# Moving the weight loads of an attention and mixture-of-experts kernel from SyncE's queue to ACT's

## What is computed

```
x = x + attention(layernorm(x), ctx)        # q = ln(x) Wq + bq; k, v from ctx; ALiBi bias; softmax; Wo
g = softmax(layernorm(x) Wg + bg); top 2, renormalised
for e in range(8):
    h = gelu(ln(x) @ W1[e] + b1[e]);  out += (h @ W2[e] + b2[e]) * combine_w[:, e]
x = x + out
```

## Time and profile before

| | us |
|---|---|
| median of 3 runs (512.02 to 512.95) | 512.09 |
| the profiled execution | 508.91 |
| its span | 507.1 |
| PE busy in the span | 419.6 |
| DVE busy | 312.6 |
| ACT busy | 232.4 |
| POOL busy | 223.7 |

### The profile page before, as it was taken

The page is one execution under the profiler, slowest core; times in us unless marked ns, Lnnn a source line. Parts: engine busy times, 40 slices in busy tenths (PEclk is TensorE's granted clock), DMA queues, the critical chain, the costliest instruction groups (busy, mean ns, idle before and its releaser), DMA issues. The chain is left out here.

```text
span 507.1 us, 16158 instructions
## 1 busy us (share of the span) xinstructions
PE 419.6 (83%) x5137; PEld 330.3 (65%) x5138; DVE 312.6 (62%) x875; ACT 232.4 (46%) x607; POOL 223.7 (44%) x305
## 2 busy tenths in 40 slices
PE   5565768897888999995179899989989998999981
PEld 2554556676666778873168677668867876777760
DVE  5357848796778777554526466636664765566560
ACT  1333636564555564563234444534543553445430
POOL 3123528887888886677602222222222232122232
PEclk9865979898989999998579999989998999999997
DMA  6574455555646535333322223113222322122110
GB/s 225 134 229 150 139 152 189 175 175 192 215 136 185 165 123 163 122 123 127 127 64 37 39 41 53 35 29 45 46 44 31 53 38 43 34 43 47 22 12 0
DMA packets 52967, 50.70 MB, mean 100 GB/s; under 512 B 22672, under 2 KB 47024, under 8 KB 52784
## 3 DMA queue, kind: packets, MB, share of 16 engines
q1 hardware_dynamic: 45192, 41.07, 27.0%
q0 software_dynamic: 7152, 8.47, 9.9%
q10 hardware_dynamic: 576, 0.53, 0.3%
HBM read 33.73 MB, written 17.50 MB: 101 GB/s over the span
## 5 line engine op out<-in xcount | busy, mean ns | idle before, releaser
L976 PE MATMUL ps<-area,wts 128*128 128x128 f16 (+1 forms) x2896 | 197.0, 243 | 0.1
L976 PEld LDWEIGHTS ps<-area,wts 128*128 (+1 forms) x2896 | 157.5, 103 | 41.0 <-issue 2.1
L976 PE MATMUL ps<-wts,area 128*128 x624 | 153.4, 330 | 2.2 <-DVE area L934 1.8
L718 ACT ACTIVATE area<-ps,late 128x128 f32<-128x128 f32 x312 | 89.2, 368 | 115.0 <-PE ps L976 115.0
L932 DVE TENSOR_SCALAR area<-area 128x512 f16<-128x512 f32 x78 | 33.0, 424 | 77.8 <-ACT area L718 77.7
L976 PE MATMUL ps<-area 128*128 128x154 f16 (+2 forms) x928 | 71.0, 236 | 12.0 <-DMA area<-qd 11.1
L976 PEld LDWEIGHTS ps<-area 128*128 128x128 f16 (+1 forms) x928 | 59.8, 107 | 21.2 <-issue 8.1
L595 POOL DMA_INDIRECT out<-o,row_id x20 | 31.6, 1579 | 95.1 <-issue 65.0
L595 POOL DMA_INDIRECT out<-xn,row_id x19 | 30.0, 1579 | 92.4 <-issue 79.8
L804 DVE TENSOR_REDUCE mx<-ps 128x3 f32<-128x462 f32 (+1 forms) x96 | 53.1, 579 | 24.3 <-PE ps L976 23.9
L621 ACT ACTIVATE area<-ps 128x512 f32<-128x512 f32 x80 | 47.3, 595 | 27.7 <-PE ps L976 25.5
(11 more groups left out here) (121 smaller groups left out, 419.1 us busy)
## 6 DMA issues: line engine op xcount, KB each, us to landing
stage<-in_w SPq DMA_DIRECT2D x32, 512.0 KB, 5.0
area<-xlist SPq DMA_DIRECT2D x39, 130.0 KB, 2.0
area<-qd SPq DMA_DIRECT2D x16, 256.0 KB, 2.7
qd<-wts SPq DMA_DIRECT2D x48, 64.0 KB, 1.9
area<-in_x SPq DMA_DIRECT2D x16, 128.0 KB, 2.3
out<-area SPq DMA_DIRECT2D x16, 128.0 KB, 1.8
xlist<-pad_rows SPq DMA_DIRECT2D x11, 130.0 KB, 2.5
area<-in_b SPq DMA_DIRECT2D x1, 1024.0 KB, 5.0
```

The costliest lines, as they stand in the source:

```text
L718: last = nc.scalar.activation(h32[par][:, c * P:(c + 1) * P], h_ps[par][m][:, f * P:(f + 1) * P], ACT.Gelu_apprx_tanh, bias=b1T[:, ds(e * ...
L976: return nc.tensor.matmul(out_, lhsT, rhs, start=start, stop=stop, skip_group_check=skip)
```

## The change

All loads of weights, the output pack and the kink tables are issued by ACT instead of SP. `load_w` is the same function with `act` in place of `sp`. In the turns it stands at the end of ACT's turn, after the second weight split; before the first turn it stands after ACT's `query(0)`. SP keeps the x loads and stores, the hops and the spare rows.

```
 SP, before the first turn, and in turn(i):
-            for u in range(2):
-                load_w(u)
             load_x(3)
-            sp.dma_start(late[:], pack_o).then_inc(s.o_in, 16)
...
                     write_q(f2)
                     read_q(f2)
-                for u in weight_units(i + 1) if i > -3 else []:
-                    load_w(u)
                 if sc is not None:
                     write_m(sc)
-                if i == 2:
-                    sp.dma_start(kinks[:], kink_in).then_inc(s.kink_in, 16)
 ACT, in turn(i), and before the first turn:
+            def load_w(u):
+                e, second, n, place = u // 4, u % 4 // 2, u % 2, u % NSTAGE
+                wait(act, S[f"w_lo{place}"], u // NSTAGE)
+                if second:
+                    act.dma_start(staged(u), w2[e, n * 512:(n + 1) * 512, :].rearrange("(c p) d -> p c d", p=P)).then_inc(S[f"w_stage{place}"], 16)
+                else:
+                    act.dma_start(stage[:, place, :], w1[e, n * P:(n + 1) * P, :]).then_inc(S[f"w_stage{place}"], 16)
...
                 for u in units[1:2]:
                     split_w_hi(u)
+                for u in weight_units(i + 1) if i > -3 else []:
+                    load_w(u)
+                if i == 2:
+                    act.dma_start(kinks[:], kink_in).then_inc(s.kink_in, 16)
...
             query(0)
+            for u in range(2):
+                load_w(u)
+            act.dma_start(late[:], pack_o).then_inc(s.o_in, 16)
             for i in range(FIRST, LAST):
                 turn(i)
```

More of the change, by code:

```diff
@@ L374, in store @@
                 sp.dma_start(out_rows[ds(first_row(t), P), :], xr[:, t % 8, :]).then_inc(s.x2_out, 16)
[L376 to L382, removed]
             def write_q(t):
```

## The result

The changed kernel is slower. Its median is 526.37 us (4 runs, 520.29 to 526.68) beside 512.06 us for the kernel before (511.12 to 512.95): a ratio of 1.027 [1.021, 1.032]. The prediction was 507.2 us, in a range of 502.0 to 514.5. Run again later beside other kernels it came to 522.17 us (6 runs, 518.22 to 525.09), 1.018 [1.013, 1.023]. The profiled execution took 526.68 us, its span is 524.8 us.

What follows compares the result with a forecast made beforehand. Before the expert loop, TensorE waits for the queries' read-back, held up by slow `md` writes behind weight loads in SyncE's queue. Stall gains less added costs summed to -4.9 us: 512.09 becomes 507.2, range 502.0 to 514.5.

Steps and rivals of the forecast that it cites:

- Turn 2: Turn 2's scores: `md` lands in 3 us, the stall shrinks by 3.0 us and the low clock behind it by 2.0.
- ACT's issue time: Turns: two issues, about 0.9 us a turn, mostly covered by ACT's idle time, except at turn 14's start: +0.5.
- About 1 us does not [fit in]: +1.0: Start-up: most data of loads ACT issues earlier fits into free engine time before first scores; +1.0, bounds 0 and +4.
- rival 3: Start-up costs the full 4 us, time 510.2; chance 0.07.
- Early turns: 0: End of turn -2: units 2 and 3 issued beside the query read, offset by freer `qd` write; 0, bounds -1 and +1.5.
- Turn 6's stall: the same mechanism: -2.2: Turn 6's scores: a quicker `md` hop removes TensorE's wait as in turn 2; -2.2 us, bounds 0 and -3.
- The kink tables, "+0.3 at most": End of turn 2: one issue more on ACT, before a turn in which TensorE waits for POOL; +0.3 taken.
- Turn 16, "+0.8 (bounds 0 and +2.5)": Turn 16: units 30 and 31, issued late beside `b2`, delay ACT's split and the tail; +0.8.
- Rival 2: Every turn: loads collide with the `md` write, using up 2.7 us to spare; 523.9, or 519.4 at half the turns; chance 0.12.
- three signs of being wrong: Steady-turn `md` at 4 us or more, new `area<-qd` waits in turns 3 to 12, first scores after 26.5 us.
- rival 1: Hops keep their length because engines are full; 514.9, or 511.0 with half the stalls' time gone; chance 0.16.

Runs made afterwards that it cites:

- experiment 4: Kernel before with SyncE's weight loads issued behind the `md` write instead of ahead of it, nothing on ACT; 507.68 us, 0.994.
- experiment 10: Kernel before with only the two first weight loads and the output pack issued by ACT, after its first query copy; 515.46 us, 1.005.
- 5: Changed kernel with start-up loads, output pack and kink tables back on SyncE, units 30 and 31 issued by ACT a turn earlier; 516.92 us, 1.012.
- 9: Kernel 5 with the units of turns -1 and 0 issued by ACT at the start of their own turn; 513.46 us, 1.001.
- experiment 2: Changed kernel with only the kink tables issued by SyncE again, behind the maxima write of turn 2; 521.44 us, 1.019.
- experiment 7: Changed kernel with only units 30 and 31 issued by ACT at the end of turn 14 instead of 15; 519.91 us, 1.012.
- 6: Kernel 5 with units of turns -1 to 12 issued by ACT behind its xnT copy, later ones by SyncE behind the `md` write; 509.73 us, 0.994.
- 12: Kernel before, SyncE's loads both behind the `md` write in early turns; from turn 3 one ahead, one behind; 509.31 us, 0.995.

## Why the prediction was wrong

**What held.** *Turn 2.* The working gave `md` 3 us to land and took 5.0 us from turn 2 (3.0 for the stall, 2.0 for the clock). The hop took 3.03 us, the turn became 5.7 us shorter, and the granted clock of 66 to 73 us went to 1.00. The mechanism was right, and experiment 4 shows that it was had without a second queue. *ACT's issue time* was taken at +0.5 in turn 14 and cost nothing: ACT idles the same 0.32 us before it copies `o_sb` at 227.49 as it did before. The issues aren't in the engine's way, since they go out while earlier activations still run.

**What failed.** Under most of the steps lies one: that `md` and the other hops get through quickly once the loads are in another queue, whenever the loads leave. By the steps of the prediction:

- *"About 1 us does not [fit in]: +1.0"* for the start-up. It was 2.9 us in the trace and 2.4 us alone (experiment 10), rival 3's case more nearly. The step summed the free time of 14.6 to 24 us and let the loads fill it. But loads issued first aren't filler. They took the engines to 0.99 in 18 to 22 us, when the hops were out, and left 0.35 free in 22 to 27, when there was nothing left to hide.
- *"Early turns: 0"*. They cost 3.3 us in turns -1 and 0, about 1.0% by experiments 5 and 9. The step looked at the queue (query read beside loads, not behind them) and assumed that ACT issues at the end of its turn. It issues before its splits begin, in turn -2 beside the queries' writes, the first load 0.4 us ahead of them:

```profile
30.42 0.39 ACTq L606 DMA_DIRECT2D stage<-in_w  x1
30.69 1.05 ACT L600 ACTIVATE wts<-stage 128x1024 f16<-128x1024 f32 x1
30.82 0.89 SPq L382 DMA_DIRECT2D qd<-wts  x2
...
36.12 0.33 SPq L396 DMA_DIRECT2D area<-qd  x1
```

  From the last write's issue (31.76) to the read-back it takes 4.36 us; before, from 28.83 to 31.15, 2.32.
- *"Turn 6's stall: the same mechanism: -2.2"*. It grew to 2.92 us (TensorE, scores at 127.65). The wait was rightly named, but the step took for granted that `md` is quick in a queue without loads. With loads 1.0 and 0.6 us ahead of it in the other queue it took 6.08 us, against 4.21 before. In this kernel the hops of turns 1, 2 and 4 take 4.4 to 6.1 us; before, those of turns -2 to 1 took 4.6 to 6.0. The long hops have moved rather than gone.
- *The kink tables, "+0.3 at most"*. Priced as an issue on ACT, they are a transfer that leaves with a weight load 0.7 us before a read-back of the queries. TensorE stood 5.46 us, turn 3 grew by 5.7 us, or turn 4 by about 3 in the repeat. Undoing it (experiment 2) cut the wait to 1.59 us but gave no measurable time.
- *Turn 16, "+0.8 (bounds 0 and +2.5)"*: 2.1 us by experiment 7, inside the bounds. The "5 to 6 us to land" beside `b2` were 7.6 for the first unit and up to 10.0 for the second.
- *Steady turns*, for which the sum has no term. Rival 2 gave them 4.5 to 9 us, and its times, 519.4 and 523.9, lie nearest to the measured 522.17 and 526.37. That nearness is in the main luck. Its collision did come: the `md` hop takes 3.25 us, mean of the last eight, instead of 1.77, and in turns 5 to 11 TensorE waits for the queries three times (2.92, 1.40 and 1.11 us) instead of once (2.19), so the 2.7 us to spare were used up there. But it priced about ten turns alike, and turns 5 to 11 are no longer than in kernels 4, 6 and 12. The loss stands mostly where rival 2 had little: in the start-up, the early turns and turns 3 and 4.

Two of the prediction's three signs of being wrong came: the first scores start at 27.27 us, after 26.5, and waits for `area<-qd` stand in turns 3, 6, 9 and 11. The third, `md` at 4 us or more in the steady turns, is met in three of the last eight hops (4.2 to 4.5 us).

The chances had the same fault: rivals 2 and 3 stood at 0.12 and 0.07 as alternatives to the forecast, and a part of what each describes came true beside its gain.

**The rule.** The forecast stood on the second queue: it gave `md` its own share. In the trace the same 8 KB, in a ring of its own, take 3.25 us with loads just ahead in ACT's ring, and 1.72 us (experiment 4) with loads 0.4 us behind them in the same ring. The Trainium skill, "DMA: Bandwidth & Descriptors", section "Issuing engines are not separate DMA queues", says that transfers run on the same 16 engines and interleave whichever engine starts them. The trace agrees. The time by the working of rival 1, 514.9, was still too low, because it let every hop keep its old length. SyncE's waits for `qd` grew from 24.3 to 29.8 us, and the hops that the loads now meet got longer.

**What stays open.** The steps of the ladder, 0.7% (9 to 6), 1.0% (5 to 9) and 0.6 to 1.5% (after to 5), are differences of measured ratios; they give no price for each single transfer, and the profiles don't show where the 0.7% lies. Taking away the start-up loads or the kink tables alone moved the time by no more than its spread, while stalls turned up in other turns. Why a stall settles in one turn and not the next is not explained. Whether the `md` write waits for the engines' time or for its completion behind the loads' data isn't separated by any run. Loads just ahead of the `md` write in SyncE's queue in the steady turns were not tried; for that queue there are only the early turns of the kernel before.

## What to carry to other kernels

Ask of a large transfer when it leaves and which small hop goes out in the next 3 us, before asking whose queue it is in. Here it paid to put it right behind the write of the hop that its queue waits for next (two lines moved on SyncE gave 0.994 [0.991, 0.997], where the new queue gave 1.018 to 1.027). Follow each hop to the turn in which it is first used before calling it critical: the maxima's hop doubled in the steady turns and those turns took no longer than in the fastest kernels. Compare the parts of a trace with those of several kernels, not with one profile before. When a change is priced as "this stall goes", list the other hops that the moved work now meets with their slack, and don't count mechanisms that can act together as alternatives.

## What the runs showed of the hardware

- ACT's transfers leave ahead of the engine's own earlier activations: loads that the program has behind the second split were issued at 57.29 and 57.72 us, the split began at 57.88. "At the end of the turn" in the program's text was 0.6 to 3.1 us before SyncE's `md` write from turn 0 on, and up to 6.1 us before it in turn -2.
- A small transfer isn't shielded by a ring of its own: 8 KB took 3.25 us (mean of the last eight, issue to read-back) with loads just ahead in the other ring, against 1.77 with the same loads some 5 us ahead in its own; the longest were 6.1 us after and 6.0 before.
- The landing of `area<-md` has no record, so whether a read-back is late has to be settled by when it is first used (at least 8.9 us after its issue in the changed kernel), not by which engines wait near it.
- The low-clock stretches followed the stalls: the granted clock was 0.52 in 66 to 73 us before and 1.00 after, 0.54 in 83 to 90 us behind the 5.46 us stall, and 0.51 in 104 to 114 us behind 4 us in which TensorE was busy for 2.0.
